# Reordering the emptying steps of a software-pipelined RWKV + FP4 feed-forward kernel: rounding chains of two tiles interleaved, PE work placed between the halves of a gate and up product

## The reference, cut to what matters

```python
# attention-like layer
r, k, v = xr @ W_r.T, xk @ W_k.T, xv @ W_v.T; g = sigmoid(xg @ W_g.T)
state = state * w + k v^T ; out = state r          # scan over time, 16 heads of 16
x = layernorm(x + layernorm_affine((out * g) @ W_o.T))
# feed-forward layer, every operand rounded to blockwise FP4 (blocks of 16)
q = lambda a: GRID[searchsorted(MID, |a / scale|)] * sign(a) * scale   # scale = max|block| / 6
h = silu(q(x) @ q(w_gate).T) * (q(x) @ q(w_up).T)                      # 704 hidden
x = layernorm(x + q(h) @ q(w_down).T)
```

## Time and profile before

| | us |
|---|---|
| median of 3 runs (567.2, 567.55, 569.61) | 567.55 |
| the profiled execution, its own time | 568.91 |
| span of the profiled execution, first to last instruction | 567.0 |
| PE busy / DVE busy / POOL busy / ACT busy | 520.9 / 508.8 / 286.1 / 260.0 |
| mean granted TensorE clock | 0.98 |

### The profile page before, as it was taken

The page is one execution under the profiler, slowest core; times in us unless marked ns, Lnnn a source line. Parts: engine busy times, 40 slices in busy tenths (PEclk is TensorE's granted clock), DMA queues, the critical chain, the costliest instruction groups (busy, mean ns, idle before and its releaser), DMA issues.

```text
span 567.0 us, 14892 instructions
## 1 busy us (share of the span) xinstructions
PE 520.9 (92%) x5169; PEld 453.7 (80%) x5169; DVE 508.8 (90%) x1535; ACT 260.0 (46%) x614; POOL 286.1 (50%) x439
## 2 busy tenths in 40 slices
PE   2769789899999999999999999999999999988775
PEld 1657568788888898988888888888988888867764
DVE  7998577999999999999999999999999999889983
ACT  3426454455444455445455544445544545432231
POOL 3246443445565555555554555555655545556232
PEclk9978789999999999999999999999999999999999
DMA  7300000000000000000000000000000000000001
GB/s 212 126 1 2 11 11 10 1 22 20 20 20 20 23 10 12 21 21 20 20 21 21 20 20 20 22 20 4 18 21 21 10 11 11 13 0 21 10 10 32
DMA packets 14046, 13.14 MB, mean 23 GB/s; under 512 B 2576, under 2 KB 13712, under 8 KB 13968
## 3 DMA queue, kind: packets, MB, share of 16 engines
q1 hardware_dynamic: 13968, 12.13, 7.0%
HBM read 7.93 MB, written 4.19 MB: 21 GB/s over the span
## 4 chain that ended last, share of the span: by engine, by line
issue 47%; POOL 40%; PE 5%; DVE 4%; ACT 2%; POOLq 1%; DMA 0%; ACTq 0%; DVEq 0%
POOL scores L410 11%; POOL rstd L392 11%; POOL hq L462 8%; POOL nmr L404 4%; POOL shift L435 3%; POOL xb L448 2%; DVE mix L1233 1%; POOL xq L419 1%; PE bank L794 1%; ACT scores L589 1%; PE bank L919 1%; PE bank L891 1%; PE bank L971 1%; PE bank L743 0%; PE bank L862 0%
## 5 line engine op out<-in xcount | busy, mean ns | idle before, releaser
L589 ACT COPY scores<-bank 128x512 f32<-128x512 f32 x128 | 68.3, 593 | 74.2 <-PE bank L794 74.2
L462 POOL TENSOR_TENSOR hq<-late,h_scale 128x704 f32<-128x704 f32 x31 | 43.2, 1392 | 96.4 <-DVE late L1092 96.4
L971 PE MATMUL bank<-down_t,hq_t 128*128 128x256 f32 x384 | 88.2, 379 | 0.9 <-ACT hq_t L665 0.8
L410 POOL TENSOR_SCALAR_AFFINE_SELECT scores<-scores 128x512 f32<-128x512 f32 x128 | 80.6, 666 | 11.2 <-ACT scores L589 11.2
L1233 DVE SCALAR_TENSOR_TENSOR mix<-shift,mu,x_t 128x128 f32<-128x128 f32 x256 | 80.9, 364 | 1.3 <-POOL shift L435 1.3
L971 PEld LDWEIGHTS bank<-down_t,hq_t 128*128 128x128 f32 x384 | 71.6, 190 | 9.6 <-issue 1.0
L419 POOL TENSOR_TENSOR xq<-x_grid,x_scale 128x256 f32<-128x256 f32 x32 | 19.9, 620 | 113.7 <-DVE x_grid L1092 113.7
L392 POOL TENSOR_TENSOR rstd<-veps,neg_half 128x1 f32<-128x1 f32 x96 | 65.2, 688 | 18.1 <-DVE veps L1180 18.0
L855 PE MATMUL bank<-gu_hi,xq_hi 128*128 128x352 f32 x256 | 71.2, 359 | 2.6 <-DVE late L1297 2.6
L891 PE MATMUL bank<-mix,proj_t 128*128 128x128 f32 x512 | 65.2, 281 | 0.1
L891 PEld LDWEIGHTS bank<-mix,proj_t 128*128 128x128 f32 x512 | 60.2, 193 | 3.5 <-issue 1.3
(11 more groups left out here) (130 smaller groups left out, 1145.1 us busy)
## 6 DMA issues: line engine op xcount, KB each, us to landing
x_tok<-in_L_attn_x_dram SPq DMA_DIRECT2D x32, 128.0 KB, 2.3
out_dram<-late_down SPq DMA_DIRECT2D x32, 128.0 KB, 1.7
late_down<-in_L_ffn_w_down_dram SPq DMA_DIRECT2D x1, 704.0 KB, 8.3
late<-in_L_ffn_w_gate_dram SPq DMA_DIRECT2D x1, 640.0 KB, 4.6
late<-in_L_ffn_w_up_dram SPq DMA_DIRECT2D x1, 640.0 KB, 6.9
scores<-in_L_attn_W_r_dram SPq DMA_DIRECT2D x1, 256.0 KB, 4.5
scores<-in_L_attn_W_v_dram SPq DMA_DIRECT2D x1, 256.0 KB, 4.6
scores<-in_L_attn_W_g_dram SPq DMA_DIRECT2D x1, 256.0 KB, 4.8
```

Source lines behind the costliest of these rows:

```text
L410: g.affine_select(out=a, in_=a, compare_op=ALU.is_ge, fill=0.0, base=0, pattern=[[0, 4], [1, P]], channel_multiplier=-1).then_inc(s_masked, 1)
L462: g.tensor_tensor(blocks(hq[:, t.c % 2, 0:HID], nb), blocks(h_grid, nb), per_block(h_scale, nb), ALU.mult).then_inc(hq_ready, 1)
L589: s.copy(scores[:, t.c % 2, 4 * q:4 * q + 4, :], src).then_inc(s_moved, 1)
L971: mm = t_.matmul(B_PA[:, 0:C], hq_t[:, t.c % 2, j], down_t[:, j], start=(j == 0), stop=(j == NH - 1))
```

## The change

Only steps 33 to 39 change.

- DVE: `xgrid` of tile s - 5, which stood at the end of a step, alternates with `hgrid`, `norm1` and `norm2` from the start. `gated(0)` moves from behind `hgrid(6)` to behind `xgrid(4)` (its wait on the rounding is relaxed to `hgrid(3)`, the last that reads `hid`). `low_x` is done for the tile whose `xgrid` ran in the same step. `norm3(0)` stands ahead of `gated(1)`, `norm3(1)` and `norm3(2)` are the last of the step, behind `last_grid(1)`.
- PE: `transpose_h` and `project_down` of tile s - 8 both run in step s, the transposes behind `gate_up(t, 0)`, the projection and then `transpose_xq` of tile s - 5 between the gate half and the up half of `gate_up(t, 1)`.
- ACT: the `xq_hi` copy is made for tile s - 5 behind `gate(t, 1)`; the `hq_t` copies are those of tile s - 8.
- POOL: `scale_x` and `rstd_of(t, 1)` stand ahead of `hq`; `rstd_of(t, 2)` is the last of the step, behind the multiplies of the last tile's halves.

```diff
@@ POOL
+                if drain:
+                    scale_x(tile(5), general)
+                    t = tile(4)
+                    if t is not None:
+                        rstd_of(t, 1, general)
                 t = tile(6 + ffn)
                 if t is not None and not (is_last(t) and drain):
...
-                t = tile(7 + ffn)
-                if t is not None and drain:
-                    rstd_of(t, 2, general)
                 t = tile(5 + ffn)
                 if is_last(t) and drain:
...
+                t = tile(7 + ffn)
+                if t is not None and drain:
+                    rstd_of(t, 2, general)
@@ ACT
                 t = tile(6 + ffn)
+                if drain:
+                    t = tile(7 + ffn) if tile(2) is None else None
                 if t is not None:
                     wait(act, h_tr, t.count(1, 1))
...
+                t = tile(5 + ffn)
+                if t is not None and drain:
+                    gate(t, 1)
+                if drain:
+                    move_xq(tile(5))
@@ PE
-            def gate_up(t, i):
+            def gate_up(t, i, only=(0, 1)):
...
-                if drain:
-                    transpose_xq(tile(5 + ffn), ffn)
-                    if tile(2) is None:
-                        project_down(tile(7 + ffn))
+                done = tile(7 + ffn) if drain and tile(2) is None else None
+                if drain and tile(2) is not None:
+                    transpose_xq(tile(5 + ffn), ffn)
...
-                if not drain:
-                    transpose_h(tile(6 + ffn), ffn, general)
+                transpose_h(done if drain else tile(6 + ffn), ffn, general)
...
-                    gate_up(t, 1)
+                    gate_up(t, 1, (0,) if drain else (0, 1))
+                project_down(done if drain else tile(6 + ffn))
                 if drain:
-                    transpose_h(tile(6 + ffn), ffn, general)
-                else:
-                    project_down(tile(6 + ffn))
+                    transpose_xq(tile(5), ffn)
+                    if t is not None:
+                        gate_up(t, 1, (1,))
@@ DVE
-                        wait(dve, hquant_step, t5.count(QN, 0))
+                        wait(dve, hquant_step, t5.count(QN, 4 - QN))
...
                     hgrid(0)
                     norm1(0)
+                    xgrid(0)
                     hgrid(1)
                     norm1(1)
+                    xgrid(1)
+                    norm1(2)
                     hgrid(2)
-                    norm1(2)
                     centred()
-                    low_x()
+                    xgrid(2)
+                    if t2 is not None:
+                        low_x(t5)
                     hgrid(3)
+                    gate_heads()
                     residual()
-                    gate_heads()
+                    xgrid(3)
                     hgrid(4)
+                    norm2(0)
+                    xgrid(4)
+                    gated(0)
+                    xgrid(5)
+                    norm2(1)
+                    xgrid(6)
+                    norm2(2)
+                    hgrid(5)
+                    next_state(0)
+                    hgrid(6)
+                    next_state(1)
                     if t2 is None:
                         add_x1()
-                    norm2(0)
-                    hgrid(5)
+                    next_state(2)
+                    low_x(tx)
+                    last_grid(0)
                     norm3(0)
...
                     gated(1)
                     last_grid(1)
+                    norm3(1)
+                    norm3(2)
                     return
```

More of the change, by code:

```diff
@@ L476, in step @@
                                         ).then_inc(last_ready, 1)
+                t = tile(7 + ffn)
+                if t is not None and drain:
+                    rstd_of(t, 2, general)
                 t = tile(4)
-                if t is not None:
+                if t is not None and not drain:
                     rstd_of(t, 1, general)
-                if not general:
+                if not general and not drain:
                     scale_x(tile(5), general)
@@ L605, in tanh_half, with move_xq @@
                                  ACT.Tanh, scale=0.5).then_inc(tanh_ready, 1)
+            def move_xq(t):
+                if t is not None:
+                    wait(act, xq_tr, t.count(1, 1))
+                    wait(act, gu_done, t.count(2, -2))
+                    s.copy(xq_hi[:, t.c % 2], B_T[:, 0:C].rearrange("p (k n) -> p k n", k=KC)
+                           ).then_inc(xq_copied, 1)
             def output(t):
@@ L622, in step @@
                     turned(tile, 0)
[L623 to L628, removed]
+                drain = draining(tile, general)
+                if not drain or tile(2) is not None:
+                    move_xq(tile(5 + ffn))
                 t = tile(1)
@@ L642, in step @@
                         tanh_half(t, g_k_done)
-                drain = draining(tile, general)
                 if not drain:
@@ L656, in step @@
                     score(t, 3)
-                t = tile(5 + ffn)
-                if t is not None and drain:
-                    gate(t, 1)
                 t = tile(6 + ffn)
+                if drain:
+                    t = tile(7 + ffn) if tile(2) is None else None
                 if t is not None:
@@ L844, in gate_up @@
                     wait(pe, xq_t_ready, t.count(1, 1))
-                for b, o in ((B_GATE, 0), (B_UP, HID)):
+                for b, o in ((B_GATE, 0), (B_UP, HID))[only[0]:only[-1] + 1]:
                     if b is B_GATE:
@@ L1328, in add_x1, with low_x @@
                         v.tensor_tensor(u2, B_PA[:, 0:C], x1[:, t7.c], ALU.add).then_inc(ln2_step, 1)
[L1330 to L1335, removed]
+                def low_x(t):
+                    if t is not None:
+                        wait(dve, xq_copied, t.count(1, 1))
+                        wait(dve, gu_done, t.count(2, -2))
+                        v.tensor_tensor(xq_lo[:, t.c % 2],
                                         B_T[:, 0:C].rearrange("p (k n) -> p k n", k=KC),
-                                        xq_hi[:, t5.c % 2].bitcast(F32), ALU.subtract
+                                        xq_hi[:, t.c % 2].bitcast(F32), ALU.subtract
                                         ).then_inc(xq_t_ready, 1)
```

## The result

The changed kernel takes 579.05 us (median of 4 runs, 578.49 to 581.12), the kernel before 567.38 in the same session: a ratio of 1.0205, 95% interval 1.0186 to 1.0224. It is slower by 2.05%; the forecast was 576.1, slower by 1.5%, with a range that ended at 579.0. The direction and the place of most of the loss are as forecast, the size is not: 11.7 us for 8.6. The 578.5 of rival B lies nearer to it, but by coincidence: its mechanism is not there (see "Why the prediction was wrong in its size").

The account below looks back on a forecast made before the run. DVE was taken to bound steps 33 to 37, latency the last 10.6 us. Terms: -1.3 (middle) + 7.4 (end's queue) + 2.5 (clock) = +8.6 us, on 567.55 giving 576.1 us; range 572.3 to 579.0.

Parts of the forecast that it names:

- rival B: Steps 35 to 37: the DRAIN rule holds, interleaved pairs save nothing and the steps keep their lengths; 578.5 us, chance 0.05.
- Part one: DVE's rounding chains: pulling apart neighbours that wait for each other saves about 0.12 us a pair, about 1.3 in step 36.
- Part three: The end, behind tile 31's rounding: tile 29's norm and output hold project_down(30), which holds tile 31's transposes; costs 7.4 us.
- Part four: The end: PE idles nine us, the granted clock falls and project_down(30) runs under the lower one; +2.5 us.
- Rival A: The end: the clock keeps its level through PE's pause; 573.6 us, slower, chance 0.10.
- Part two, step 34: Tile 31's masks wait behind rstd_of(25, 2), PE's list behind them holds DVE some 3 us; the step costs +0.9 us.
- Part two, steps 33 and 35: The walk of the new order through these steps: +0.2 us in step 33, -0.85 us in step 35.
- C: The middle steps give far more, tile 31's rounding ending 6.2 us earlier; 568.8 us with the clock kept, no change, chance 0.06.
- D: The end: tile 29's norm and output precede tile 31's second half, the 7.4 us chain never forms; 566.3 us, chance 0.04.

Follow-up runs that it names:

- e1: The changed kernel with ACT's hq_t copies of tile 30 put back ahead of output(29): 572.51 us, ratio 1.0081 to the kernel before.
- e2: The changed kernel with tile 29's norm3(1), norm3(2) ahead of last_grid(1) on DVE and rstd_of(29) ahead of tile 31's second multiply on POOL: 575.33 us, ratio 1.0127.
- e3: The changed kernel with the edits of e1 and e2 together: 570.75 us, ratio 1.0047 to the kernel before.
- e10: The kernel before with only the change's order of the end on DVE, POOL and ACT, nothing interleaved: 577.35 us, ratio 1.0162.
- e4: The changed kernel with 78 idle transposes ahead of project_down(30) on PE: 577.18 us, ratio 1.0166 to the kernel before.
- e5: The changed kernel with 30 idle transposes in step 34, between the sums and the attention output of tile 31: 577.86 us, ratio 1.0163.
- e6: The changed kernel with POOL's masks of tile 31 done in step 33, ahead of scale_x(28): 575.45 us, ratio 1.0124 to the kernel before.
- e11: e9 with POOL's scale_x made to wait for hgrid(6): 570.34 us, ratio 1.0043 to the kernel before.
- e9: The changed kernel with the edits of e3 and e6: 566.07 us, ratio 0.9967 to the kernel before.
- e7: The changed kernel with POOL's rstd_of(t, 1) moved behind its hq multiply: 582.86 us, ratio 1.0246 to the kernel before.

## Why the prediction was wrong in its size

- **Part one, the interleaving.** Right where nothing disturbs it: step 36 became 1.11 us shorter for a forecast of 1.3. Neighbours of two chains overlap in it as in the earlier trace rows (in the changed kernel one runs from 538.69 to 539.58 and the next starts at 539.50), so rival B is out, near as its number came. No run puts the interleaving alone back, so that step 36's gain is its doing is read from these rows. The Trainium skill, VectorE: DVE Perf Modes, section "The DRAIN you can't avoid", which the prediction set against the change, also says that a next operation that is not held starts earlier, so it spoke against it less than the prediction had it; the trace agrees, 0.08 us early.
- **Part three, the queue at the end.** Right: +9.36 us with the clock for 9.9, and e1, e2, e3 and e10 show that each link (DVE's and POOL's place of tile 29's norm, ACT's of its output) holds as forecast. e10 makes the queue out of the kernel before alone.
- **Part four, the clock at the end.** Right: 2.5 us by e4, +2.5 forecast. Rival A is out.
- **Part two, step 34, is the step that failed.** It had the masks ending at 512.9 (512.74 measured) and PE waiting for them, but costed PE's list behind them at the upper clock, +0.9 in all. The pause was 3.86 us and the clock fell in it. Part four had read from the earlier trace rows that the clock was down 3.3 us behind the last matmul, and used that for the end; the same reading was not held against this pause. The term measured +3.7 in the profile, +2.2 to +2.3 in those of e1 to e4; e5 gives the clock's share as 1.5 to 2.9, and e6 shows that without the wait the step is 11.03, under the 12.72 of before. With the clock kept (e5) the step is 13.50, +0.78 for +0.9: the walk itself came out, and its clock was the term put at nothing.
- **Part two, steps 33 and 35** were sized too low, +1.05 for +0.2 and +0.08 for -0.85. The walk took each duration from rows in which the neighbours on POOL were different ones. `scale_x` moved from beside `gated(1)` and the next reduction to beside `hgrid(6)`: 0.3 us on DVE and 0.6 on POOL in each of four steps (e11). And the wait of `hgrid(0)` on POOL's multiply, in the code of `hgrid`, was not walked: 0.45 and 0.51 us. Three stretches of 0.3 and the two waits make 1.9 us, for a miss of 2.0 in steps 33, 35 and 36. With e1's to e4's step 34 the differences of the whole profile would sum to 11.5 us, near the 11.7 of the medians (an estimate from these profiles).
- Rivals C and D are out. What C asked for, a middle that gives over 5 us, is not there even in e6: 1.6. D asked for `norm3(2)` of tile 29 ahead of `last_grid(1)`; it runs at 559.39, behind it.

The Trainium skill, SBUF — State Buffer, section "SBUF: two separate sides", says that a DVE operation with two SBUF inputs and a GpSimd operation that reads SBUF take one port pair in turns, each for its whole instruction. By that rule, `scale_x` costs 0.62 plus what is left of the DVE instruction that it meets; at 532.65 that is 0.79 us of the one that started at 532.56 and took 0.88, which makes 1.41, an estimate. The trace agrees within 0.15 us: `scale_x` took 1.26 there, and 0.62 in e11.

## What to carry to other kernels

In a pipeline of engines that each work in order, a closing chain is set by what stands ahead of its links on every engine: follow one tile's norm, output and copies through all queues before moving one of them, since one place on ACT was worth 7.0 us of 567 here (e1). Where a new wait leaves the matmul engine idle, cost what stands behind it at the lower clock too, at every such pause and not only the longest, and ask whether that engine is the bound there: in e9 the lower clock cost nothing in a step that DVE bounds. A duration taken from a row belongs to the neighbours that it ran beside; when an instruction is moved, ask what runs beside it in its new place.

## What was not expected of the hardware

The clock fell behind pauses shorter than the 3.3 us of the earlier trace rows: in e1 in the second of two of 1.1 and 1.4 us, so that five idle transposes took 1.33 us for 0.71, and in e9 behind a single one of 2.16 us, behind which it stayed up in e6. The cost of one and the same pause differs between executions: step 34 took 16.4 us in one profile of this order and 15.0 in four others. A 128x64 DVE instruction of 0.22 us took 1.38 beside POOL's 128x704 multiply (e7).
